# Next row's statistics taken one body ahead, and o's statistics half a step earlier, in a fused Mamba block and FFN

## The reference

```python
x = x + layernorm(mamba(layernorm(x)))
x = x + layernorm(ffn(layernorm(x)))
```

## Time and profile before

| | us |
|---|---|
| median of 3 runs | 1581.29 (1579.59 to 1582.81) |
| profiled execution | 1581.47 |
| its span, first to last instruction | 1579.7 |

### The profile page before, as it was taken

The page is one execution under the profiler, slowest core; times in us unless marked ns, Lnnn a source line. Parts: engine busy times, 40 slices in busy tenths (PEclk is TensorE's granted clock), DMA queues, the critical chain, the costliest instruction groups (busy, mean ns, idle before and its releaser), DMA issues.

```text
span 1579.7 us, 27006 instructions
## 1 busy us (share of the span) xinstructions
PE 1347.9 (85%) x9264; PEld 1216.6 (77%) x9264; DVE 1292.9 (82%) x1963; ACT 1217.7 (77%) x2635; POOL 1135.2 (72%) x1351
## 2 busy tenths in 40 slices
PE   6665898898979889898988989898898979888897
PEld 4344788887868878787888878788887868877797
DVE  6999897878879787887978788797878879787852
ACT  6564778888787888878788887878888787887663
POOL 4656587787868778686877868687786868777621
PEclk8575899999999999999999999999999999998999
DMA  7401010101010010111101010100101111010100
GB/s 263 138 28 34 29 29 22 42 29 43 29 42 29 22 42 29 42 29 40 30 23 42 29 43 29 41 30 22 42 29 43 29 42 29 22 36 29 29 3 16
DMA packets 39165, 63.17 MB, mean 40 GB/s; under 512 B 5248, under 2 KB 19456, under 8 KB 38928
## 3 DMA queue, kind: packets, MB, share of 16 engines
q10 hardware_dynamic: 18944, 33.83, 6.9%
q1 hardware_dynamic: 19984, 26.02, 5.0%
HBM read 55.38 MB, written 4.46 MB: 38 GB/s over the span
## 4 chain that ended last, share of the span: by engine, by line
ACT 27%; DVE 27%; POOL 19%; PE 14%; issue 11%; SPq 0%; DMA 0%; POOLq 0%; DVEq 0%; ACTq 0%
DVE S L1681 10%; POOL S L582 8%; DVE acc L1695 7%; PE hP L764 5%; POOL Glo L655 5%; ACT dA L1256 4%; DVE hP L1710 4%; ACT Rw L1456 3%; ACT L1456 2%; ACT Rw L1391 2%; ACT hP L1343 2%; ACT o L1288 2%; ACT Rw L1450 2%; DVE stats L1666 1%; PE sT L800 1%
## 5 line engine op out<-in xcount | busy, mean ns | idle before, releaser
L1681 DVE TENSOR_TENSOR_SCAN S<-dA,S 128x512 f32<-128x512 f32 x512 | 620.4, 1212 | 148.0 <-ACT dA L1256 73.6
L582 POOL TENSOR_TENSOR S<-X,Bs 128x1024 f32<-128x1024 f32 x255 | 609.6, 2391 | 172.3 <-PE sT L800 141.7
L1256 ACT ACTIVATE dA<-delta,A 128x255 f32<-128x255 f32 x1024 | 445.6, 469 | 228.9 <-DVE S L1681 227.5
L776 PE MATMUL fP<-Ghi,w_h 128*128 128x256 f32 x1736 | 439.0, 292 | 0.7 <-DVE o L1754 0.6
L777 PE MATMUL fP<-Glo,w_h 128*128 128x256 f32 x1736 | 418.5, 280 | 0.0
L800 PE MATMUL sT<-ident,S 128*128 128x128 f32 x2048 | 333.2, 290 | 92.4 <-DVE acc L1695 89.8
L1695 DVE SCALAR_TENSOR_TENSOR acc<-sT,CT,acc 128x512 f32<-128x512 f32 x480 | 348.0, 728 | 38.6 <-PE sT L800 38.0
L800 PEld LDWEIGHTS sT<-ident,S 128*128 128x128 f32 x2048 | 252.6, 149 | 137.2 <-DVE S L1681 74.1
L776 PEld LDWEIGHTS fP<-Ghi,w_h 128*128 128x128 f32 x1736 | 327.2, 188 | 4.0 <-ACT Rw L1450 1.2
L777 PEld LDWEIGHTS fP<-Glo,w_h 128*128 128x128 f32 x1736 | 327.3, 189 | 0.4
L655 POOL TENSOR_TENSOR Glo<-Rw,Ghi 128x1024 fp32r<-128x1024 f32 x86 | 202.6, 2356 | 60.3 <-ACT Ghi L1462 46.8
(11 more groups left out here) (271 smaller groups left out, 2267.4 us busy)
## 6 DMA issues: line engine op xcount, KB each, us to landing
Bs<-b_rows ACTq DMA_DIRECT2D x128, 256.0 KB, 3.2
xh<-in_x SPq DMA_DIRECT2D x16, 256.0 KB, 3.9
xt<-in_x SPq DMA_DIRECT2D x16, 256.0 KB, 4.1
out<-x SPq DMA_DIRECT2D x15, 256.0 KB, 3.1
Rw<-in_w SPq DMA_DIRECT2D x4, 512.0 KB, 4.2
Rw<-in_h SPq DMA_DIRECT2D x4, 512.0 KB, 5.4
delta<-in_h SPq DMA_DIRECT2D x3, 512.0 KB, 4.4
X<-in_h SPq DMA_DIRECT2D x3, 512.0 KB, 7.2
```

The lines of the kernel that those rows point to most:

```text
L582: pool.tensor_tensor(s[:, :, :], X[par][:, :, :], row[:, None, :].broadcast_to([P, DT, T]), ALU.mult).then_inc(scan_pool.sem, 1)
L776: pe.matmul(dst, w[:, i, cols_], hi[:, i, :], start=(j == 0), stop=False)
L1256: a = act.activation(dA[half][:, i, 1:], delta[par][:, d, 1:], ACT.Exp, scale=A[:, d * N + n:d * N + n + 1])
L1681: a = dve.tensor_tensor_scan(pair, dA[half][:, :, :].rearrange("p d t -> p (d t)"), pair, 0.0, ALU.mult, ALU.add)
```

## The change

- `x_stats` and `x_aggr` leave `head_vec` and get a sequence of their own, `ahead_vec`.
- In bodies 1 to 13 VectorE takes the statistics of row c+2 in half step 13, and GpSimd makes its factors in half step 20, before the end's sum. Rows 1 and 2 are still done in half step 3 of bodies 0 and 1.
- SyncE loads row c+2 before the tail's stream and before the output store. It still waits for `hn` of row c+1.
- o's statistics follow the add of o in half step 4.

```diff
+        ahead_vec = Steps(sem("ahead_vec"), ["x_stats", "x_aggr"])
         head_vec = Steps(sem("head_vec"),
-                         ["x_stats", "x_aggr", "tap0", "tap1", "tap2",
+                         ["tap0", "tap1", "tap2",
                           "sum", "res", "delta"])
...
+        def rows_ahead(c, hs, late):
+
+            return ([c + 1] if c < 2 and hs == 3 else []) + ([c + 2] if 1 <= c < CHUNKS - 2 and hs == late else [])
...
+                if head and c + 2 < CHUNKS:
+                    sp.wait_ge(head_act.sem, head_act.at(c + 1, "hn"))
+                    sp.dma_start(xh[:, :, :], x_in[c + 2]).then_inc(xh_in.sem, 16)
                 if tail:
...
-                if head and not (isinstance(c, int) and c + 2 >= CHUNKS):
-                    sp.wait_ge(head_act.sem, head_act.at(c + 1, "hn"))
-                    sp.dma_start(xh[:, :, :], x_in[c + 2]).then_inc(xh_in.sem, 16)
...
-                if hs == 3:
-                    pool.wait_ge(head_vec.sem, head_vec.at(h, "x_aggr"))
-                    head_factors(h)
...
+                    for h in rows_ahead(c, hs, 20):
+                        pool.wait_ge(ahead_vec.sem, ahead_vec.at(h, "x_aggr"))
+                        head_factors(h)
                     if end and hs != 13:
                         end_step(c - 2, par, hs)
...
-                if hs == 3:
-                    dve.wait_ge(xh_in.sem, xh_in.at(h, "landed"))
-                    stats(head_vec, h, ("x_stats", "x_aggr"), xh, hstat, hmv)
...
                     dve.tensor_tensor(o[:, :, :], ring(1 - fp, "out")[:, :, :], o[:, :, :],
                                       ALU.add).then_inc(tail_vec.sem, 1)
-                if hs == 5:
                     dve.wait_ge(tail_vec.sem, tail_vec.at(f, "o_add"))
                     stats(tail_vec, f, ("o_stats", "o_aggr"), o, tstat, tmv)
...
+                    for h in rows_ahead(c, hs, 13):
+                        dve.wait_ge(xh_in.sem, xh_in.at(h, "landed"))
+                        stats(ahead_vec, h, ("x_stats", "x_aggr"), xh, hstat, hmv)
                     if tail and hs == 15:
                         split_input(c - 1, 1 - par)
```

More of the change, by code:

```diff
@@ L1646, in _ @@
         def _(dve):
-            start(dve, first_vec, last_vec, head_vec, scan_vec, acc_vec, tail_vec, end_vec)
+            start(dve, ahead_vec, first_vec, last_vec, head_vec, scan_vec, acc_vec, tail_vec, end_vec)
             for half in range(2):
@@ L1851, in _ @@
             wait_first(first_vec, "X1")
+            dve.sem_inc(ahead_vec.sem, ahead_vec.per_chunk)
             dve.sem_inc(head_vec.sem, head_vec.per_chunk)
```

## The result

The changed kernel took 1539.03 us (median of 4 runs, 1534.39 to 1545.22) beside 1582.05 us (1579.59 to 1582.86) for the kernel before: ratio 0.9733, 95% interval 0.9696 to 0.977. The prediction said 1573 us, range 1561 to 1581: the sign was right, the size far too small. The profiled execution took 1537.83 us, 43.6 less than that of before.

A forecast was written before the change was run, and what follows sets the result against it. No engine alone bounds the kernel; the chain runs through GpSimd's factors, with TensorE late next. 13 x 0.76 + 0.9 = 10.8 us gained and 2.9 lost to the clock: 1581.3 - 10.8 + 2.9 = 1573.4, said 1573, range 1561 to 1581.

The forecast's parts named there:

- The start of o's factors: GpSimd, half steps 3 to 4: o's moments ready at 599.9 instead of 602.3, so o's factors start then.
- The statistics in half step 13 and the factors in half step 20: VectorE's 0.95 us fits a 3.18 us wait, GpSimd's 3.48 a 4.73 us wait: no cost.
- The load worth nothing: SyncE: the row's load, issued some 46 us earlier at 0.47 us issue cost, gains or costs nothing.
- The long stretch over hidden layer 1: TensorE at low clock there costs about 1.4 us a body.
- What is late next. TensorE: Half steps 3 to 10: TensorE limits ScalarE's copy of tile 6, so a body gains 0.76 us, not 2.
- The clock: Four bodies more with hidden layer 1's long low stretch, three fewer with the output product's: +5.6 - 2.7 = +2.9 us.
- Body 1: No hidden layer 2 bounds it; o's moments come about 1.8 us earlier; gain -0.3 to 1.7, taken as 0.9.
- Body 15: Already without the factors; earlier o's moments bring it to the same TensorE bound: 0 to 0.5 us, taken as 0.
- C: Clock gives more: u's and some output products at full clock, 1557 to 1563 us; chance 0.22.
- B: Clock takes it back: long low stretch meets hidden layer 1 in about every second body, 1580 us; chance 0.15.
- D: Slower: long low stretch over hidden layer 1 in 13 bodies, 1589 us, decided from 8 upward; chance 0.10.
- E: Hidden anyway: TensorE full for the whole stretch, the 0.76 us slack not real, 1581 us; chance 0.08.

The follow-up runs named there:

- after_again: The changed kernel, unaltered, timed again in a later session beside the kernel before: 1554.96 us, ratio 0.9826.
- the filled kernels: Kernel before and changed kernel with unread products cut to fit both TensorE gaps (before_warm2, after_warm2): 1566.15 and 1534.85 us.
- o_only: The kernel before with only o's statistics moved to half step 4: 1579.44 us, ratio 0.999.
- before_warm2: The kernel before with unread TensorE products, 7 ahead of the output product and 11 ahead of u's: 1566.15 us.
- o_warm: The kernel before with only o's statistics moved, plus 7 and 11 unread products in TensorE's two gaps: bodies of 91.06 us.
- after_warm2: The changed kernel with 7 unread products in each of TensorE's gaps, ahead of the output product and of u's: 1534.85 us.
- after_pad1: The changed kernel with one short unread ScalarE copy in half step 11 of bodies 2 to 14: 1563 us.
- after_pad: The changed kernel with three short unread ScalarE copies in half step 11 of bodies 2 to 14: 1573 us.
- after_out: The changed kernel with 7 unread products ahead of the output product only: 1535.89 us, ratio 0.9719.
- pad_out: The changed kernel with three unread ScalarE copies in half step 11 and 7 unread products ahead of the output product only: 1550.62 us, ratio 0.9803.

## Why the prediction was wrong

**Right.** The chain through GpSimd's factors. The start of o's factors: +8.5 worked, +8.4 measured. The statistics in half step 13 and the factors in half step 20 hidden, with 1.25 us to spare worked and 1.35 measured. The load worth nothing, shown by itself. TensorE next in line, at tile 6: 0.76 worked, 0.72 where the output product is at low clock. The long stretch over hidden layer 1 at 1.4 us (1.5 measured), and up to 1.6 for the one over the output product once TensorE bounds (1.5 measured).

**The step that failed** is "What is late next. TensorE", with its **0.76 us**. The bound was read from a body whose output product ran at low clock. Once TensorE bounds half steps 3 to 10, those 1.5 us are on the path themselves, so the step has two values: 0.7 with a low output product (after_again, body 6), 2.3 with a full one (the filled kernels). I had the second in the text, as what one low stretch less gives back, but gave it to three bodies only.

**The second failure** is the count in "The clock", +2.9 us with the wrong sign. I took from one body that shorter bodies meet the long stretch more often, in four bodies more. The first measurement had it once (body 8), as before; the output product was low in two bodies and u's products in one, where before nearly all had both. The account for bodies 2 to 14 closes with the measured prices: order at full clock 13 x 2.29 = 29.8; low stretches before, 13 x 0.95 + 1.4 = 13.8, after 2 x 1.5 + 1.1 + 1.5 = 5.6; together 38.0 of the 38.3 measured. In the later session the profiled execution is 1581.47 - 1566.92 = 14.6 us below that of before, inside the stated range, but it is the longest of six, and the medians differ by 1579.98 - 1554.96 = 25.0. How the low stretches fell in the first measurement was luck as far as these runs tell: between the two sessions it was worth 16 us. The first failure stands without it, as the filled kernels show.

**The Trainium skill**, "TensorE: Matmul & The Clock Gate" (What's actually happening), was drawn on for the gate's free-running schedule, by which the steady pattern would break up. The first measurement does not look so, with a low stretch that begins at +51 to +53 in every body from 2 to 14 but the eighth; that of the later session does, with five kinds of bodies in turn. No run here tells what the schedule is.

**Body 1** was taken at 0.9 us and brought 1.9 (85.11 to 83.20); o_only has it at 82.66, so it is o's statistics that bring it. With the output product at full clock on both sides they bring 0.9, as worked (83.92 in before_warm2, 83.04 in o_warm); the other 1.0 stays open, since o_only has the output product of body 1 at low clock (5.71 us) and is the shortest of all. **Body 15** and what follows was taken at 0 and brought 3.8 (158.8 to 155.0). The order is worth little of it: 0.1 where the output product is at low clock (158.7 in after_again), 0.6 where both are at full clock (156.1 in before_warm2, 155.5 in after_warm2).

**The rivals.** C was nearest, with u's products at full clock. Its size was wrong: 1.3 to 2 us on top of the order's share in half of the bodies, where it was 1.5 + 1.1 = 2.6, in ten of 13. Its ground does not hold either: TensorE's gap before u did shrink, to 1.84, but in body 6 of after_again it is 1.85 and the products still take 3.58. B and D are refuted in both sessions, and E by the filled kernels, 31 us apart. D's "from 8 such bodies upward" was also reckoned short: 8 x 1.4 = 11.2 only uses up the 10.8, and to be 3.2 us slower it takes ten.

**Open.** What decides which pattern an execution of the unfilled kernel falls into. A new session is enough to change it with the same program; the sessions were on different chips, and that of the first measurement is not on record, so chip and session are not told apart. That 0.2 or 0.5 us a body (after_pad1, after_pad) changes it is likely but not shown, for want of the unpadded kernel beside them. Also not tried: filling TensorE's time ahead of hidden layer 1, which would be the last low stretch with a price.

## What to carry to other kernels

If a bound is read off a stretch whose TensorE clock is low, work the sum twice, at either level: an engine that becomes the bound puts its clock on the path, and a change can be worth three times as much with a full clock as with a low one. Where low stretches recur in a loop, write down what each place costs and compare bodies by it, not totals; totals of the same program can differ by a per cent. A short gap in TensorE's stream filled with products that nobody reads, no longer than the gap, made the changed kernel steady as well as fast (1535.1 to 1537.4 us). In the kernel before, a filler that overran its gap by a microsecond took back nearly all that the shorter one brought (1579 us against 1566).

## What had not been expected of the hardware

- Behind a gap of 2.07 us in TensorE's stream the output product ran at low clock in most bodies of before (5.41 us), and in the changed kernel in 2 bodies of 13 or in 9, by the session. With the gap cut to 0.51 us no body from 2 on of before_warm2, after_warm2, after_out or pad_out had a low stretch there (3.72 us). The gap alone does not decide it: o_only has the full 2.07 us and 3.72 us from body 2 on.
- The changed kernel without fillers stood at 1539 us in one session and 1555 in another, each time with several lengths of body. Its version with one 128x64 copy more in a body, which costs 0.15 to 0.2 us, stood at 1563 in a third.
- A 7 us low stretch costs 0 at +52 to +59 and 1.5 us at +66 to +73 of the same body.
